# Expert stage: normalisation on ScalarE, clamps ahead of pair sums on GpSimd, one transpose copy placed earlier

## The reference

```
x = x + 0.5 * ffn(layernorm(x))
ffn(h): q = h @ W_q.T, split in two halves and 4 heads of 64
        sim = q . keys                       (2 x 4 heads x 64 keys)
        top 8 of each half; all 64 sums; top 8 of these: scores, indices
        w = silu((h . down_embed[index]) * softmax(scores))
        out = sum of w * up_embed[index] + silu(h @ W_up.T) @ W_down.T
layernorm(x) = (x - mean) / sqrt(var + 1e-5)    over 256 features, no weights
```

## Time and profile before

| | us |
|---|---|
| median of 3 runs | 4577.6 (4576.49 to 4580.62) |
| profiled execution, its own time | 4583.77 |
| its span, first to last instruction | 4582.0 |
| mean granted TensorE clock | 0.949 of full |

### The profile page before, as it was taken

How to read it: one execution, slowest core, us unless ns; L and a number is a source line. 1 busy time by engine, 2 the same in 40 slices (tenths; PEclk the granted TensorE clock), 3 DMA queues, 4 the chain that set the end, 5 groups by cost and what they waited for, 6 DMA issues and landing times. The chain is left out here.

```text
span 4582.0 us, 89009 instructions
## 1 busy us (share of the span) xinstructions
PE 4003.9 (87%) x29160; PEld 3388.7 (74%) x29160; DVE 3499.3 (76%) x9021; ACT 2890.6 (63%) x7413; POOL 2058.2 (45%) x1554
## 2 busy tenths in 40 slices
PE   5999999889869999999995889999999979796879
PEld 4787778778747777777774777777777857686757
DVE  7888888888657777777775888888888858455667
ACT  4777777777558888888883777777777733220123
POOL 5777777777520111111101777777777721011200
PEclk8999999999979999999997999999999989898989
DMA  1000000000010000000001000000000012359332
GB/s 57 15 15 14 14 14 14 14 14 14 10 41 11 16 16 21 12 21 21 11 11 62 10 15 15 14 14 15 14 15 19 10 49 92 123 197 251 99 93 80
DMA packets 175252, 179.33 MB, mean 39 GB/s; under 512 B 9552, under 2 KB 167536, under 8 KB 174832
## 3 DMA queue, kind: packets, MB, share of 16 engines
q1 hardware_dynamic: 174832, 174.40, 12.2%
HBM read 98.87 MB, written 75.50 MB: 38 GB/s over the span
## 5 line engine op out<-in xcount | busy, mean ns | idle before, releaser
L371 POOL TENSOR_TENSOR f_grid<-f_sim 128x1024 f32<-128x1024 f32 x512 | 963.9, 1904 | 0.0
L705 DVE SCALAR_TENSOR_TENSOR f_p_u<-f_grid,f_te,f_p_dot 128x512 f32<-128x512 f32 x1024 | 720.7, 751 | 173.5 <-PE f_p_dot L106 106.4
L1349 ACT ACTIVATE a_ex<-a_p_s,a_mneg 128x128 f32<-128x128 f32 x2048 | 718.5, 403 | 211.5 <-DVE a_mneg L1394 211.5
L713 DVE SCALAR_TENSOR_TENSOR f_q<-f_p_u,f_rz,f_grid 128x512 f32<-128x512 f32 x1024 | 720.3, 747 | 0.0
L379 POOL TENSOR_TENSOR f_q<-f_q 128x1024 f32<-128x1024 f32 x256 | 611.5, 2392 | 203.2 <-ACT f_q L594 198.6
L575 ACT ACTIVATE f_grid<-f_grid,f_negm 128x1024 f32<-128x1024 f32 x512 | 558.5, 1141 | 0.0
L497 PE MATMUL f_p_y<-f_wdn,f_hs 128*128 128x256 f32 x2048 | 524.8, 415 | 0.0
L1349 ACT ACTIVATION_READ_ACCUMULATOR a_ex<-a_p_s,a_mneg 128x1 f32 x2048 | 497.2, 243 | 0.0
L502 PE MATMUL f_p_y<-f_eup,f_wT 128*128 128x256 f32 x2048 | 473.1, 379 | 0.0
L497 PEld LDWEIGHTS f_p_y<-f_wdn,f_hs 128*128 128x128 f32 x2048 | 418.8, 210 | 68.4
L502 PEld LDWEIGHTS f_p_y<-f_eup,f_wT 128*128 128x128 f32 x2048 | 390.1, 190 | 58.9
(11 more groups left out here) (369 smaller groups left out, 10050.1 us busy)
## 6 DMA issues: line engine op xcount, KB each, us to landing
x_f<-f_yt SPq DMA_DIRECT2D x64, 256.0 KB, 2.2
f_xt<-x SPq DMA_DIRECT2D x32, 256.0 KB, 2.8
a_xt<-x_f SPq DMA_DIRECT2D x16, 512.0 KB, 4.2
x_a<-a_yt SPq DMA_DIRECT2D x16, 512.0 KB, 2.9
f_xt<-x_a SPq DMA_DIRECT2D x32, 256.0 KB, 2.8
c_xt<-x_f SPq DMA_DIRECT2D x16, 512.0 KB, 4.6
x_c<-c_yt SPq DMA_DIRECT2D x16, 512.0 KB, 3.1
b1p_xt<-x_c SPq DMA_DIRECT2D x16, 512.0 KB, 4.4
```

Of the source, the lines that this page charges most:

```text
L371: g_grid.mark(pool.tensor_tensor(grid[v][:, hd, :].rearrange("p (i j) -> p i j", i=XROWS), sx[:, hd, :].unsqueeze(2).to_broadcast([P, XROW ...
L705: d_mask.mark(dve.scalar_tensor_tensor(out=p_u[e][:], in0=grid[v][:, hd, half_e], scalar=te[:, v, hd, TOP - 1:TOP], in1=p_dot[:, half_e], ...
L713: d_mul.mark(dve.scalar_tensor_tensor(out=q[v][:, hd, half_e], in0=p_u[e][:], scalar=rz[:, v, hd:hd + 1], in1=grid[v][:, hd, half_e], op0= ...
L1349: last = act.activation(ex[t.step % 2][:, i, n, :], p_s[i][:, n, :], ACT.Exp, bias=mneg[:, i, n:n + 1], accum_out=z[t.step % 2][:, i, n:n ...
```

## The change

Four edits, all in `expert_ffn`:

- DVE's `normed` is gone. ACT computes h = Identity(rstd * x + shift) with two activations per turn, with per-partition scale and bias, placed between hidden(t,0) and weights(t,0), for turn t+2.
- POOL computes shift = -mean * rstd after each root, with two instructions of 128x2 and waits between them.
- POOL's order: scores(t+1,1,(0,)) and clamps(t,1) come ahead of summed(t,1,0).
- ACT's turned(t-1,1,0) moves from `step(t)`, behind exps(t,1,(0,1)), into next_exps, ahead of listed(t,1).

```diff
+        shift, a_h = m.sbuf("shift", 2, 2, V), m.track("a_h")
+        g_shift = m.track("g_shift", "product", "shift")
...
+                def root(t):
+
+                    k = t.step % 2
+                    norm.root(pool, t)
+                    norm.g_ln.wait(pool, t, "rstd")
+                    g_shift.mark(pool.tensor_tensor(shift[:, k, 0, :], norm.mv[:, k, :, 0], norm.rstd[:, k, :], ALU.mult), "product")
+                    g_shift.wait(pool, t, "product", alone=True)
+                    g_shift.mark(pool.tensor_scalar(shift[:, k, 1, :], shift[:, k, 0, :], -1.0, None, ALU.mult), "shift")
...
-                    summed(t, 1, 0)
-                    clamps(t, 1)
                     if after:
                         scores(t + 1, 1, (0,))
+                    clamps(t, 1)
+                    summed(t, 1, 0)
                     summed(t, 1, 1)
                     if (t + 3).exists(last=count):
-                        norm.root(pool, t + 3)
+                        root(t + 3)
...
                 def turn_h(t):
-                    norm.d_h.wait(pe, t)
+                    a_h.wait(pe, t)
...
+                def normed(t):
+
+                    k = t.step % 2
+                    g_shift.wait(act, t)
+                    slot_wait(act, s_ld, t)
+                    if (t - 1).exists():
+                        t_hT.wait(act, t - 1)
+                    for v in range(V):
+                        last = act.activation(h[:, v, :], xt[t.step % 4][:, v, :], ACT.Identity,
+                                              bias=shift[:, k, 1, v:v + 1], scale=norm.rstd[:, k, v:v + 1])
+                    a_h.mark(last)
...
                     exps(t, 0, (2, 3))
+                    if (t - 1).exists():
+                        turned(t - 1, 1, 0)
                     listed(t, 1)
...
                     exps(t, 1, (0, 1))
                     if before:
-                        turned(t - 1, 1, 0)
                         turned(t - 1, 1, 1)
                     exps(t, 1, (2, 3))
                     if after:
                         similar(t + 1, 1)
                     hidden(t, 0)
+                    if later:
+                        normed(t + 2)
                     weights(t, 0)
...
-                            if later:
-                                normed(t + 2)
```

More of the change, by code:

```diff
@@ L392, in clamps @@
                     g_tail.mark(pool.tensor_tensor(u8[:, v], u8[:, v], tail[:, v], ALU.mult), f"use{v}")
-                norm.root(pool, first)
-                norm.root(pool, first + 1)
+                def root(t):
[5 more added lines that the diff above has]
+                    g_shift.mark(pool.tensor_scalar(shift[:, k, 1, :], shift[:, k, 0, :], -1.0, None, ALU.mult), "shift")
+                root(first)
+                root(first + 1)
                 pairs(first, 0)
@@ L398, in _ @@
                 pairs(first, 1)
-                norm.root(pool, first + 2)
+                root(first + 2)
                 scores(first, 1, range(HEADS))
@@ L611, in next_exps @@
                     exps(t, 0, (2, 3))
+                    if (t - 1).exists():
+                        turned(t - 1, 1, 0)
                     listed(t, 1)
+                normed(first)
                 turn_h(first)
@@ L616, in _ @@
                 similar(first, 1)
+                normed(first + 1)
                 turn_h(first + 1)
@@ L649, in front @@
                     norm.statistics(dve, t)
[L651 to L654, removed]
                 def turned(t):
@@ L743, in _ @@
                 front(first)
-                normed(first)
                 front(first + 1)
@@ L750, in _ @@
                 best(first, 1)
-                normed(first + 1)
                 front(first + 2)
```

## The result

The change makes the kernel faster by 4.7%. The median is 4362.3 us (4360.5 to 4366.7, four runs) against 4577.1 (4572.1 to 4580.6, four runs) before: a ratio of 0.953 with a 95% interval of 0.952 to 0.955. The profiled execution took 4360.5 us, span 4358.3.

What follows compares the result with a forecast made beforehand. A ring of waits through DVE, POOL and ACT was taken as the bound. Pitch 33.58 + 0.59 (loop's end) + 0.2 (clock fall) = 34.4 against 37.36, times 62 saves 184 us: 4394, range 4365 to 4480.

Steps and rivals of the forecast that it cites:

- (a): Normalisation off DVE: two instructions of 0.73 or 2.79 us go per turn; v=1 starts 14.74 us after v=0, not 17.30.
- (b): ACT copies the first half some 2.9 us sooner; PE's gap of 2.37 and ACT's wait of 1.18 go.
- (c): Two Identity activations on ACT ahead of the silus: 1.0 us for both, bounds 0.6 and 1.2, hidden.
- the ring: Chain of waits through DVE, POOL and ACT that sets a turn's length: 36.49 us before, 33.58 without waits after.
- the slower rival: Each Identity makes ACT switch tables, two loads of 1.28 us more per turn: 4599 us; chance 0.03.
- (d): Two small 128x2 products on POOL, about 0.6 us (0.4 to 1.5), in its idle time: price 0.
- (e): On POOL, clamps ahead of pair sums: the clamp comes 0.49 us sooner in each turn.
- the loop's end: Once in four turns DVE has 3.01 us of issue ahead of v=0, not 0.64: 0.59 per turn, left in.
- The prologues: Work outside the 62 pitches of the two expert stages: claimed to change by under 2 us.
- PE and ACT as the bound: PE and ACT bound each other at 35.4 us a turn: saves 120, 4457 us; chance 0.22.
- the gap that only moves: PE still waits ahead of the wT transposes: saves 50 to 108 us, about 4500; chance 0.08.
- the plain ring: No clock fall, pitch 34.17: 4380 us; with the loop's end hidden too, 33.6: 4344; chance 0.12.

Runs made afterwards that it cites:

- norm_moved: Changed kernel with the normalisation back on DVE, but earlier in DVE's order, ahead of best(t+1,0): 4424.7 us, 0.967 of the kernel before.
- no_copy: Changed kernel with ACT's copy of the first half of transposes back behind the two grid exps: 4513.9 us, 0.986 of the kernel before.
- no_clamp: Changed kernel with POOL's old order, pair sum ahead of the clamp: 4404.0 us, 0.963 of the kernel before.
- copy_alone: Kernel before with only ACT's copy of the first half of transposes moved earlier, normalisation still on DVE: 4600.8 us, 1.006 of the kernel before.
- stt_norm: Changed kernel with the normalisation back on DVE, its scale written as SCALAR_TENSOR_TENSOR with both inputs in SBUF: 4554.0 us, 0.996 of the kernel before.

## Why the prediction was wrong, step by step

**Right.** (a) The floor of v=0 to v=1 is 14.74 in the ordinary turn, as forecast, and norm_moved shows that the hold by POOL was rightly read from 2.79 beside 0.73. How often it mattered was not: "Of four turns, two lose it in one way" counts long L195, but in before one ends the wait for v=1 only in the turn behind each loop end (the turn of 500.39 is one), five of twenty in either stage; in the others p_dot comes last. (b) L495's wait for ACT is gone, and ACT's own wait for the second half; PE's clock is 0.99 in the stage. no_copy puts the edit at some 150 us in the presence of the others. (c) The pair of Identities takes 1.09 and delays ACT by 0.99, where 1.0 was taken, and the ring hides it. PE's wait for ACT's silu was to grow by 0.2 to 0.4 a turn and didn't: it is 6.3 us in 25 waits, 0.25 each, and was 5.1 in 21 before, 0.24 each. ACT's last silu of v=0 ends 17.3 after v=0 and not 18.1, mostly since the moved copy took its own 0.57 along, which the sum had left in. What PE gained now goes into waits for DVE's tail, 0.5 each in the ordinary turns. The mean in the trace from 100 to 1000 us (busy, mean ns) and the table loads, still two a turn:

```profile
L569 ACT ACTIVATE f_h<-f_xt,f_shift,f_rstd 128x256 f32<-128x256 f32 x52 | 28.2, 592 | 0.0
L590 ACT ACT_TABLE_LOAD x26 | 33.4, 1283 | 0.5
L611 ACT ACT_TABLE_LOAD x26 | 33.4, 1283 | 0.5
```

So the slower rival is out: none stands at L569. But the argument against it rested on a reading that was wrong: "30 loads, all at L588" was one row of two, and the kernel before has 29 more at L567, the small exps (100 to 1200 us):

```profile
L567 ACT ACT_TABLE_LOAD x29 | 37.2, 1283 | 0.5
```

Two loads a turn were there before and are there after. The Trainium skill advises to keep multiplies and adds on VectorE ("ScalarE: Activation LUTs", Rules for kernel authors). From that advice and the rows the prediction had worked out a loss of 17 us for this part; with the other two edits in, it is worth 181. (d) The shift costs POOL 0.65 where 0.6 was taken, and no one waits. (e) 0.49 of the ring per turn: L621 starts 13.93 after v=1, and no_clamp's pitch is 0.49 above that of after.

**The steps that failed** are two terms of the sum; the mechanism stood. The first is the loop's end: "Once in four turns, at the loop's end, DVE has 3.01 of issue ahead of v=0 where other turns wait 0.64: 2.37, or 0.59 per turn, and I leave it." The size of one is right (3.03 in after). The count is not: the loop has five ends in a stage of 31 pitches, not one in four, because the first and the last groups of four stand outside of the hardware loop, unrolled, and have none. That was to be read from the kernel before: five of its turns in the first stage have 3.0 to 3.3 us ahead of v=0 (the profile puts two of them down to ACT, as it does the 3.32 of the earlier trace rows). 5 x 2.37/31 = 0.38 a pitch, 0.21 less than the 0.59: 13 us of the gain. What remains of the mean is 0.21 in the first stage, the turns behind such an end with PE's clock fall above all (the 0.2 I had). 33.57 + 0.38 + 0.21 = 34.16, which is what the timelines have. In the second stage the clock falls only twice and the pitch is 34.06; that and 37.34 and 37.30 in place of 37.36 before make another 2.6 us.

**The second term**, and the larger one, was "The prologues change by under 2 us." The ring was costed for 62 pitches, the two ends of each stage at nothing. In fact the ramp gave 2.2 and the last turn 6.5 in the first stage, 8.9 together in the second: 17.7 in all. The last turn's 4.7 is the copy again: PE had waited there twice as long as in the middle (before, PE from 1200 to 1230 us), because the last turn has no next one whose `similar` matmuls would keep PE busy ahead of L484 (its timeline has none there, and PE stands from 1209.7 to 1214.4),

```profile
PE f_p_wT L484 <- ACT f_wT L582: 4.7, 1, 4.7
```

and its granted clock was 0.50 from 1214 to 1218. In after the gap there is 1.33 and the clock stays at 1.00. DVE's last v=1 in the kernel before:

```profile
1226.09 1.41 DVE L705 SCALAR_TENSOR_TENSOR f_p_u<-f_grid,f_te,f_p_dot 128x512 f32<-128x512 f32 x2 [6.26 <-PE f_p_dot L106]
```

and in after:

```profile
1120.64 1.42 DVE L728 SCALAR_TENSOR_TENSOR f_p_u<-f_grid,f_te,f_p_dot 128x512 f32<-128x512 f32 x2 [1.54 <-PE f_p_dot L106]
```

183.5 + 13.0 + 2.6 + 17.7 = 216.8, which is the 216.7 that the two stages of the traces lost; the medians differ by 214.8. Both errors leaned the same way, and either alone would have left the time inside the range. The range itself was put a little narrower than its own words: half of the way from 4380 to 4344 is 4362, not 4365.

**Rivals.** PE and ACT as the bound (4457), the gap that only moves (4500) and the table switches (4599) are all refuted by the ring of 33.57. The low one, "the plain ring", comes nearest in time but not in cause: the clock fall it leaves out is there, behind six of ten loop ends, and the loop's end isn't hidden. What no part of the prediction saw is how badly the edits do alone. It treats (a) and (b) as gains in different turns, which would make copy alone a gain; it is a loss of 29.

## What to carry to other kernels

Price an edit to a ring in the presence of the others: of two waits that end about together, taking away one shows nothing or, where it brings one engine's work forward onto an instruction that another's then waits out, a loss. Count an event that comes once per pass of a loop from the trace (here five waits of 3.0 to 3.3 us), not from the unroll factor, and cost the first and last turn by themselves, since they lack work that the middle has. An instruction that takes 0.7 in one turn and 2.8 in another may be held and not slow: look at what the neighbouring engines run at its two ends, and try it at another time before moving it to another engine.

## What the runs showed of the hardware that I had not expected

- A DVE TENSOR_SCALAR from SBUF of 0.41 us that starts while a GpSimd TENSOR_TENSOR of 2.38 us runs ends with it: 1.80 and 2.51 us in copy_alone, one L195 per pair sum. A pair of them meets two back-to-back sums with 4.2 us in place of 0.73.
- A SCALAR_TENSOR_TENSOR with both inputs in SBUF is held alike (mean 1653 ns in stt_norm). One with an input in PSUM isn't (at most 773 ns in after), nor is a BATCH_NORM_STATS2 from SBUF (at most 421).
- A pass of the hardware loop costs DVE 3.0 us of issue ahead of v=0, where an ordinary turn waits 0.65; eight fewer passes gave 27 us.
- Equal gaps of PE don't always bring its clock down: behind ten loop ends of after, with gaps of 2.78 to 2.92 us, the granted clock fell to 0.50 six times and stayed at 1.00 four times.
- An Identity activation with a pointer for scale and one for bias takes 592 ns at 128x256, hardly less than the 600 of a 128x512 one without pointers.
